# Queries spread into the score operand by transfers, expert choice and places later, in an attention and mixture-of-experts kernel

## The reference, cut to what matters

```
x = x + attention(layernorm(x), context)        # 16 heads of 16 channels; q and k are rms-normalised
x = x + experts(layernorm(x))                   # 8 experts, the best 2 of each token

probs = softmax(layernorm(x) @ gate_w.T); topw, sel = top_k(probs, 2); topw /= sum(topw)
out   = sum over the 2 chosen experts of topw * (silu(g) * u) @ w2,   g, u = split(x @ w1, 2)
```

## Time and profile before

| what | us |
|---|---|
| median of 3 runs (541.93 to 543.87) | 543.46 |
| the profiled execution's own time | 539.4 |
| its span | 537.6 |
| attention part with all engines in step, 59 to 302 us of the span | 243 |
| draining and the plan, to the first load of a slot at 340.89 | 39 |
| expert part, to about 505 | 164 |
| last stage | 33 |

### The profile page before, as it was taken

The page is one execution under the profiler, slowest core; times in us unless marked ns, Lnnn a source line. Parts: engine busy times, 40 slices in busy tenths (PEclk is TensorE's granted clock), DMA queues, the critical chain, the costliest instruction groups (busy, mean ns, idle before and its releaser), DMA issues.

```text
span 537.6 us, 14646 instructions
## 1 busy us (share of the span) xinstructions
PE 435.5 (81%) x4120; PEld 390.2 (73%) x4120; DVE 413.3 (77%) x1359; ACT 320.1 (60%) x934; POOL 303.4 (56%) x531
## 2 busy tenths in 40 slices
PE   1879899899999999999999861499999999999100
PEld 1668778787877887788878651399999999998000
DVE  7448998999999999999998965176777776766384
ACT  5367778777876787777777620265656666565000
POOL 6634377777777777777776646134445443544200
PEclk9879999999999999999999985599999999999655
DMA  7231442222222222223231114524344343431599
GB/s 225 65 113 43 132 142 75 81 79 80 78 75 82 75 84 74 85 65 89 68 95 53 51 41 129 148 73 131 116 124 130 116 128 119 122 116 60 182 404 351
DMA packets 49559, 60.51 MB, mean 113 GB/s; under 512 B 7615, under 2 KB 43082, under 8 KB 49482
## 3 DMA queue, kind: packets, MB, share of 16 engines
q1 hardware_dynamic: 38026, 38.00, 24.3%
q0 software_dynamic: 6528, 16.86, 9.1%
q10 hardware_dynamic: 4928, 4.72, 2.5%
HBM read 32.86 MB, written 23.27 MB: 104 GB/s over the span
## 4 chain that ended last, share of the span: by engine, by line
PE 68%; DVE 13%; DMA 5%; issue 5%; POOL 3%; SPq 3%; ACT 2%; POOLq 0%; DVEq 0%; ACTq 0%
PE bank L1117 13%; PE bank L1118 11%; PE bank L1119 11%; PE bank L1335 4%; DMA we_l<-expert_out 4%; PE bank L1125 3%; PE bank L1177 3%; PE bank L1231 2%; PE bank L1227 2%; PE bank L1229 2%; PE bank L1228 2%; PE bank L1150 2%; DVE late L835 2%; PE bank L1364 2%; PE bank L1365 2%
## 5 line engine op out<-in xcount | busy, mean ns | idle before, releaser
L527 POOL DMA_INDIRECT expert_out<-probs,late x72 | 70.0, 972 | 93.1 <-ACT probs L720 92.0
L457 POOL DMA_INDIRECT sorted_rows<-row,place_i x64 | 65.9, 1030 | 36.2 <-POOL row L451 25.3
L564 ACT CAST qp_h<-bank 32x256 f16<-32x256 f32 x128 | 46.4, 363 | 31.4 <-PE bank L1150 29.0
L841 DVE TENSOR_TENSOR qp_l<-bank,qp_h 32x256 f16<-32x256 f32 x128 | 52.9, 413 | 4.9 <-ACT qp_h L564 1.9
L1117 PE MATMUL bank<-we_h,xt_h 128*128 x144 | 53.6, 372 | 0.1
L1075 DVE SCALAR_TENSOR_TENSOR probs<-xn,late,bank 128x128 f32<-128x128 f32 x72 | 25.0, 348 | 35.6 <-ACT xn L708 35.6
L708 ACT ACTIVATE xn<-bank 128x176 f32<-128x176 f32 x72 | 22.8, 317 | 42.0 <-PE bank L1119 42.0
L1118 PE MATMUL bank<-we_l,xt_h 128*128 x144 | 47.2, 328 | 0.0
L1119 PE MATMUL bank<-we_h,xt_l 128*128 x144 | 47.1, 327 | 0.0
L1067 DVE TENSOR_TENSOR xt_l<-bank,xt_h 128x256 fp32r<-128x256 f32 x72 | 30.6, 425 | 20.3 <-ACT xt_h L702 16.1
L1335 PE MATMUL bank<-ident,late 128*128 128x128 f32 x144 | 30.7, 296 | 17.4 <-DMA late<-sorted_rows 15.7
(11 more groups left out here) (199 smaller groups left out, 1602.5 us busy)
## 6 DMA issues: line engine op xcount, KB each, us to landing
late<-sorted_rows SPq DMA_DIRECT2D x72, 129.0 KB, 2.1
we_f<-w_exp SPq DMA_DIRECT2D x32, 152.0 KB, 2.4
v_bd<-v_sb SPq DMA_DIRECT2D x128, 34.0 KB, 1.9
ctx_in<-ctx_t SPq DMA_DIRECT2D x32, 128.0 KB, 2.3
we_h<-expert_out SPq DMA_DIRECT2D x8, 512.0 KB, 6.8
we_l<-expert_out SPq DMA_DIRECT2D x8, 512.0 KB, 15.5
x<-x SPq DMA_DIRECT2D x3, 1024.0 KB, 5.8
out<-we_h ACTq DMA_DIRECT2D x8, 256.0 KB, 13.0
```

What stands on the lines that cost most here:

```text
L457: pool.indirect_dma_start(sorted_rows, bass.IndirectOffsetOnAxis(ap=place_i[:, t.slot // 2, k, t.par:t.par + 1], axis=0), row[:, k, t.slot ...
L527: pool.indirect_dma_start(expert_out, bass.IndirectOffsetOnAxis(ap=hs[:, r, D:D + 1].bitcast(U32), axis=0), y_sb[:, r % YRING, :], None, b ...
L564: act.copy(q_part(qp_h, t, g), q_bank(g)).then_inc(S["q_h_ready"], 1)
L841: dve.tensor_tensor(q_part(qp_l, t, g), q_bank(g), q_part(qp_h, t, g), ALU.subtract).then_inc(S["q_l_ready"], 1)
```

## The change

The four-part writes of `q_hi` and `q_lo` become one instruction each, of 128 partitions and 256 elements, into a new buffer `q_hl`; SyncE then spreads high and low part together with four transfers, one per group, into the score operand, whose order of dimensions is new. `score_max` waits for these transfers and has 16 matmuls with 64 stationary columns each in place of 8 with 128. On VectorE the negated maxima come straight behind `find_max`, `q_lo` comes ahead of `normalise` and of layer norm 1's statistics, `choose` moves from the end of an even turn into the middle of the following odd turn, and `route` one turn on. On TensorE `count_rows`, on GpSimd `send` and on SyncE `spread_v` come one turn later too, and the pipeline has one turn more. The comments on engines in the diff are added here.

```diff
-LAST = NT + 6
+LAST = NT + 7
...
-    qp_h = sb("qp_h", [P, 2, NB, KC, NQ, L], F16)
-    qp_l = sb("qp_l", [P, 2, NB, KC, NQ, L], F16)
+    qp = sb("qp", [P, 2, NQ, 2, KC, NB, L], F16)
+    q_hl = sb("q_hl", [P, 2, D], F16)
...
+        def spread_q(t):                       # SyncE
+            need_alone(sp, sp_passed, S["q_l_ready"], t.n + 1)
+            need_alone(sp, sp_passed, S["scored"], t.n - 1)
+            if t.n == 0:
+                sp.wait_ge(q_cleared, 1)
+            for g in range(NQ):
+                part = slice(g * 2 * HD, (g + 1) * 2 * HD)
+                sp.dma_start(qp[part, t.par, g, :, :, :, :].rearrange("p n c b l -> p (n c b l)"),
+                             q_hl[part, :, :].rearrange("p n x -> p (n x)")).then_inc(q_spread[t.par], 16)
...
         def turn(j, s):                        # SyncE
+            if Tile(j, s - 1).live:
+                spread_q(Tile(j, s - 1))
             if Tile(j, s + 2).live:
                 load_ctx(Tile(j, s + 2))
             if Tile(j, s + 1).live and (not isinstance(j, int) or j * SKEW + s + 1 >= 2):
                 load_weights(Tile(j, s + 1))
-            if Tile(j, s).live:
-                spread_v(Tile(j, s))
+            if Tile(j, s - 1).live:
+                spread_v(Tile(j, s - 1))
...
-            if Tile(j, s - 6).live:            # GpSimd
-                send(Tile(j, s - 6))
+            if Tile(j, s - 7).live:
+                send(Tile(j, s - 7))
...
         def q_hi(t):                           # ScalarE
             act.wait_ge(S["q_transposed"], t.n + 1)
-            if t.first:
-                act.wait_ge(q_cleared, 2)
-            need(act, S["scored"], t.n - 1)
-            for g in range(NQ):
-                act.copy(q_part(qp_h, t, g), q_bank(g)).then_inc(S["q_h_ready"], 1)
+            if t.n >= 1:
+                act.wait_ge(q_spread[1 - t.par], (t.n + 1) // 2 * 16 * NQ)
+            act.copy(q_hl[:, 0, :], kq_bank[:, 0:D]).then_inc(S["q_h_ready"], 1)
...
         def q_lo(t):                           # VectorE
-            dve.wait_ge(S["q_h_ready"], NQ * t.n + NQ)
-            need(dve, S["scored"], t.n - 1)
-            for g in range(NQ):
-                dve.tensor_tensor(q_part(qp_l, t, g), q_bank(g), q_part(qp_h, t, g), ALU.subtract
-                                  ).then_inc(S["q_l_ready"], 1)
+            dve.wait_ge(S["q_h_ready"], t.n + 1)
+            dve.tensor_tensor(q_hl[:, 1, :], kq_bank[:, 0:D], q_hl[:, 0, :], ALU.subtract
+                              ).then_inc(S["q_l_ready"], 1)
...
                 find_max(tile(2))              # VectorE's turn
-            if ahead:
-                n = j * SKEW + s + 2 if isinstance(j, int) else None
-                ln1_stats(ahead, {2: x_second, 8: x_third, 9: x_rest}.get(n))
-            if tile(2).live:
                 neg_max_hi(tile(2))
             if tile(3).live:
                 invert_sums(tile(3))
             if tile(2).live:
                 neg_max_lo(tile(2))
+            if tile(1).live:
+                q_lo(tile(1))
             if tile(3).live:
                 normalise(tile(3))
             if ahead:
+                n = j * SKEW + s + 2 if isinstance(j, int) else None
+                ln1_stats(ahead, {2: x_second, 8: x_third, 9: x_rest}.get(n))
                 ln1_mean(ahead)
-            if tile(1).live:
-                q_lo(tile(1))
             if tile(4).live:
                 ln2_norm(tile(4))
             if tile(3).live:
                 att_lo(tile(3))
             if s % 2 == 1 and tile(5).live:
-                route(tile(5), tile(4), (s - 5) // 2 % 2)
+                a = tile(5)
+                a.first = isinstance(j, int) and a.n == 0
+                choose(a, tile(4), (s - 5) // 2 % 2)
+            if s % 2 == 0 and tile(6).live:
+                route(tile(6), tile(5), (s - 6) // 2 % 2)
...
-            if s % 2 == 0 and tile(4).live:    # last in VectorE's turn, behind residual
-                a = tile(4)
-                a.first = isinstance(j, int) and a.n == 0
-                choose(a, tile(3), (s - 4) // 2 % 2)
...
-            pe.wait_ge(S["q_h_ready"], NQ * t.n + NQ)        # score_max, TensorE
+            pe.wait_ge(q_spread[t.par], (t.twins + 1) * 16 * NQ)
...
-                        ins = pe.matmul(score_bank[:, at:at + P], flat(qp_h[:, t.par, b, c, 2 * gh:2 * gh + 2, :]),
-                                        flat(kp[:, t.par, 0, b, c, :, :]), start=True, stop=True)
+                        for m in range(2):
+                            ins = pe.matmul(score_bank[m * L:(m + 1) * L, at:at + P], qp[:, t.par, 2 * gh + m, 0, c, b, :],
+                                            flat(kp[:, t.par, 0, b, c, :, :]), start=True, stop=True)
...
-            pe.wait_ge(S["q_l_ready"], NQ * t.n + NQ)        # score
...
-                    q_h, q_l = (flat(q[:, t.par, b, c, :, :]) for q in (qp_h, qp_l))
+                    q_h, q_l = (qp[:, t.par, :, n, c, b, :] for n in range(2))
...
-            if s % 2 == 1 and tile(5).live:                  # TensorE's turn
-                count_rows(tile(5).pair, (s - 5) // 2 % 2, static and i == 5)
+            if s % 2 == 0 and tile(6).live:
+                count_rows(tile(6).pair, (s - 6) // 2 % 2, static and i == 6)
```

More of the change, by code:

```diff
@@ L224, in k_parts @@
         return kp[:, t.par, part].rearrange("p b c q l -> p (c q) b l")
[L226 to L231, removed]
     x_first, x_second, x_third, x_rest = sem("x_first"), sem("x_second"), sem("x_third"), sem("x_rest")
@@ L239, in build_in @@
     we_loaded = [sem(f"we_loaded{p}") for p in range(2)]
+    q_spread = [sem(f"q_spread{p}") for p in range(2)]
     v_spread = [sem(f"v_spread{p}") for p in range(2)]
@@ L518, in _ @@
         assert done[0] == SETUP_POOL, done[0]
-        for q in (qp_h, qp_l):
-            pool.memset(q[:, :, :, :, :, :].rearrange("p u b c g l -> p (u b c g l)").bitcast(F32), 0.0
-                        ).then_inc(q_cleared, 1)
+        pool.memset(qp[:, :, :, :, :, :, :].rearrange("p u g n c b l -> p (u g n c b l)").bitcast(F32), 0.0
+                    ).then_inc(q_cleared, 1)
         turns_sp(pool, turn)
@@ L654, in turn @@
             if tile(1).live:
-                t = tile(1)
-                t.first = isinstance(j, int) and t.n == 0
-                q_hi(t)
+                q_hi(tile(1))
             if tile(2).live:
@@ L1129, in tr_x @@
             need(pe, S["xt_l_ready"], t.n)
-            if t.slot % 2 == 0:
+            if t.slot % 2 == 1:
                 need(pe, R["filled_new"], t.pair - 2)
@@ L1138, in tr_k @@
             pe.wait_ge(S["kn_ready"], t.n + 1)
-            need(pe, S["q_l_ready"], NQ * t.n)
+            need(pe, S["q_l_ready"], t.n)
             for c in range(KC):
```

## The result

The changed kernel took 549.3 us (median of 4 runs, 547.45 to 550.71), the kernel before, beside it, 543.7: a ratio of 1.0109, 95% interval 1.0071 to 1.0147. I had forecast 536.3, between 530 and 543. The forecast was wrong, and so was its side.

A forecast was written before the change was run, and what follows sets the result against it. TensorE was taken to bound one turn and VectorE the other. Two turns save 0.60 us, 13.5 times: -8.1; filling +0.5, draining +0.4: -7.2 us, from 543.46 to 536.3, range 530 to 543.

The forecast's parts named there:

- layer norm 1's mean: On VectorE, the mean comes 0.65 us later; GpSimd's two turns then take 17.45 us, just below TensorE's 17.56.
- my sum: GpSimd's loop over two turns, counted from `tr_k`: 6.6 + 8.05 + 1.15 + 1.65 = 17.45 us.
- Choice: `choose` in the odd turn's middle is covered, so `k_lo` is in time and TensorE's 18.4 us of waits go.
- `score_max`: On TensorE, 16 narrow matmuls in place of 8 cost +0.45 us a turn, other end 0.
- Maxima: Maxima negated straight behind `find_max` end TensorE's wait at `tr_max`: -0.11 us a turn.
- Transfers: SyncE's query transfers land 1.9 us after issue, hidden ahead of `score_max` with 0.2 to 0.7 us to spare: 0 us.
- Filling: While the pipeline fills, one longer `score_max` falls on the path: +0.5 us.
- Draining: At the pipeline's end, clock kept -1.7 us, one more `send` +3.25: sum +0.4, bounds -1 and +3.5.
- GpSimd's idle bits: Rival: the 0.24 to 0.29 us before GpSimd's L413 are sequencer work, no waits; 542.5 us, chance 0.15.
- two turns at 17.9 or more: Sign against the forecast: two turns stay at 17.9 us or more with GpSimd full; forecast 17.5.
- GpSimd with hardly an idle bit other than for layer norm 1's mean: Sign for the forecast: GpSimd's only remaining idle time of note is its wait for that mean.

The follow-up runs named there:

- e17: The changed kernel without further edit, run a third time, on chip E: 538.5 us, ratio 0.9965 to before.
- e18: The changed kernel with layer norm 1's statistics straight behind `find_max` and `q_lo` behind the mean, as before, on chip E: 533.3 us, ratio 0.9859.
- e5: The kernel before, unchanged, profiled once more on chip B: one run, 542.98 us.
- e14: The changed kernel with the front half of VectorE's turn as before and `weights_lo` ahead of `send`, on chip D: ratio 1.0185 to before.
- e1: The kernel before with only `score_max` changed to 16 matmuls of 64 stationary columns, on chip A: ratio 1.0067.
- e3: The kernel before with only `choose`, `route`, `count_rows` and `send` placed later as in the changed kernel, on chip A: ratio 0.9960.
- e4: The changed kernel with `spread_v` back at its old place in SyncE's order, on chip A: 556.5 us, ratio 1.0246 to before.
- e11: The changed kernel with `q_lo` back behind layer norm 1's mean, on chip C: 535.6 us, ratio 0.9931 to before.
- e15: The kernel of e14 profiled once more: one run, 551.82 us.
- e6 to e8: `send` moved last in GpSimd's turn, in the changed kernel, the kernel before, and the kernel of e3, on chip B: ratios 1.0904, 1.0429, 1.1114 to before.
- e12: The changed kernel with the front half of VectorE's turn as before, the same edit as e18, on chip C: 535.0 us, ratio 0.9914 to before.
- e10: The kernel before with `weights_lo` ahead of `send` in GpSimd's turn, on chip C: ratio 1.0006.
- e13: The changed kernel without further edit, run again on chip D: 550.4 us, ratio 1.0171 to before.

## Why the prediction was wrong, step by step

**The step that failed** is the one on layer norm 1's mean: "Count from the start of `tr_k` at 139.17: `qk_rms` at 145.76 is 6.6 us in". The size of the delay was right, 0.60 us measured (3.09 - 2.49) for 0.65. What was wrong is the point that I counted from. In the profile of before TensorE was busy, and `tr_k` started at 139.17, 1.20 us behind the start of `k_scale`, which ScalarE's timeline of before has at 137.97:

```profile
137.97 0.47 ACT L628 ACTIVATE late<-bank,r_qk 128x256 f32<-128x256 f32 x1 [0.43 <-POOL r_qk L415]
```

Once TensorE is not the bound, `tr_k` starts 0.53 behind `k_scale`, but `find_max` doesn't come earlier: it starts 3.50 behind `k_scale` in before (141.47 - 137.97) and 3.51 in e17. So the loop doesn't go through the start of `tr_k`. It goes from `k_scale` through the work behind it on ScalarE (softmax, `row_copy`, `e_gap`, `k_hi`) to `k_lo`, `xt_lo` and `find_max`. One turn of that loop in e17, ScalarE, VectorE and GpSimd:

```profile
136.31 0.47 ACT L631 ACTIVATE late<-bank,r_qk 128x256 f32<-128x256 f32 x1 [1.83 <-POOL r_qk L421]
145.22 0.47 ACT L631 ACTIVATE late<-bank,r_qk 128x256 f32<-128x256 f32 x1 [0.98 <-POOL r_qk L421]
154.61 0.47 ACT L631 ACTIVATE late<-bank,r_qk 128x256 f32<-128x256 f32 x1 [1.50 <-POOL r_qk L421]
```

```profile
139.82 1.22 DVE L845 TENSOR_REDUCE bank<-bank 128x16 f32<-128x1024 f32 x1
```

```profile
142.90 0.22 POOL L419 TENSOR_SCALAR veps<-mean_var 128x1 f32<-128x1 f32 x1 [0.87 <-DVE mean_var L825]
144.20 0.19 POOL L419 TENSOR_SCALAR ms_eps<-sumsq 128x2 f32<-128x2 f32 x1
...
152.26 0.19 POOL L419 TENSOR_SCALAR veps<-mean_var 128x1 f32<-128x1 f32 x1
...
153.54 0.22 POOL L419 TENSOR_SCALAR ms_eps<-sumsq 128x2 f32<-128x2 f32 x1
```

`k_scale` to `find_max` 3.51, to the mean at GpSimd 3.08, to `qk_rms` 1.30, to the next `k_scale` 1.02: 8.91 us. The next turn, 145.22 to 154.61, is GpSimd's own, 9.39.

In the terms of my sum, from `tr_k` at 136.84 to `tr_k` at 155.14: 7.36 to `qk_rms` at 144.20, where I had 6.6; 8.06 to the next layer norm, where I had 8.05; 1.28 to its `qk_rms` for 1.15; 1.60 to `tr_k` for 1.65. That is 18.30 us for my 17.45, and the first term makes 0.77 of the difference: 0.67 by the start (0.53 in place of 1.20), 0.15 by 1.30 for the layer norm in place of 1.15, less 0.06 by 3.08 for the mean in place of 3.14. The mean over ten pairs is 18.27, against the 17.56 that I forecast. Over 13.5 pairs of turns that is 9.6 us, more than the whole gain that I had forecast.

The turns show the same. Before has 8.54 us from `k_scale` at 137.97 to that at 146.51, and so 9.62 for the turn with `choose` at its end. After the change these are 8.91 and 9.39 in e17: what the moved choice gives, the later mean takes back. With the old order the first is 8.47, and two are 17.82 (e18).

**Late signals** were no step of mine: the only profile that I had shows none. One sign was there, and I carried it over without asking for its cause: the median of the runs of before lay 4 us above the profiled execution, about what late signals cost that kernel (3.6). That they are those 4 us isn't shown. They turn e17's 0.35% gain into the loss of the result, as after's `k_scale` shows, with turns of 9.52 and 9.20 us:

```profile
148.52 0.47 ACT L631 ACTIVATE late<-bank,r_qk 128x256 f32<-128x256 f32 x1 [0.73 <-POOL r_qk L421]
158.04 0.47 ACT L631 ACTIVATE late<-bank,r_qk 128x256 f32<-128x256 f32 x1 [1.34 <-POOL r_qk L421]
167.24 0.47 ACT L631 ACTIVATE late<-bank,r_qk 128x256 f32<-128x256 f32 x1 [0.73 <-POOL r_qk L421]
```

Why the changed kernel loses 12 us by them and before 3.6 is shown in part. ScalarE's `k_scale` in e5:

```profile
156.16 0.48 ACT L628 ACTIVATE late<-bank,r_qk 128x256 f32<-128x256 f32 x1 [0.44 <-POOL r_qk L415]
164.97 0.47 ACT L628 ACTIVATE late<-bank,r_qk 128x256 f32<-128x256 f32 x1 [0.44 <-POOL r_qk L415]
174.60 0.47 ACT L628 ACTIVATE late<-bank,r_qk 128x256 f32<-128x256 f32 x1 [0.43 <-POOL r_qk L415]
```

Its turns are 8.81 and 9.63. The one with `choose` at its end takes as long as in before without late signals (9.62), for VectorE is busy without a break with `choose`, `k_lo` and `xt_lo` up to `find_max`, 2.4 us behind the end of `score_max`, longer than its signal is ever late there (1.4); only the other turn can grow. In after no `choose` covers it, and both grow. Besides, in after `q_hi` starts 1.73 behind the end of `tr_q`, and behind it in VectorE's queue stand `q_lo` and the mean (at GpSimd 155.65, 5.59 behind `score_max`; in e17 161.20 - 156.15 = 5.05). But e14, with the mean ahead of `q_lo`, loses as much, and e1, whose narrow matmuls cost 0.02 us a turn by themselves (below), has 18.59 for two turns against e5's 18.30. What else is in it stays open.

The other steps:
- **Choice**: right on the waits. 18.4 us became 0.9 (e3) and 0.2 (after); e17 has 3.9, 12 times 0.3, for a `k_lo` that itself waits for ScalarE and no longer stands behind `choose`. Alone it did not shorten the turns (e3).
- **`score_max`**: +0.45 a turn was wrong, the other end of my bounds right. e1 shows it alone, since its `tr_x` (L1134) is as in before:

```profile
149.32 0.38 PE L1134 MATMUL bank<-ident,xn 128*128 128x128 f32 x2
149.63 0.64 PE L1166 MATMUL bank<-late,qp_h 128*64 128x128 f16 x16
150.10 1.07 PE L1178 MATMUL bank<-v_bd,probs 128*64 128x34 f32 x32
```

From `score_max` to `weigh` 16 narrow matmuls take 0.47 us where the eight took 0.54, from `tr_x` to `score_max` it is 0.31 where before has 0.22 (147.82 to 148.04): +0.02 a turn in all. By the Trainium skill, page "TensorEngine Tiling (Array Packing)", section "Key Properties", different tiles run weight loads and matmuls in parallel, and a change of the tiling mode drains the engine. The trace agrees with both: twice as many matmuls take no longer, and the 0.09 us move from ahead of `weigh`, where before changes its mode, to ahead of `score_max`, where after does.
- **Maxima**: right. e17's bias product starts at 159.66 and `tr_max` at 159.89, 0.23 apart where before had 0.34.

```profile
155.14 0.66 PE L1140 MATMUL bank<-ident,late 128*128 128x128 f32 x4 [0.55 <-ACT late L631]
...
156.15 0.64 PE L1163 MATMUL bank<-late,qp 128*64 128x128 f16 x16
...
159.66 0.39 PE L1122 MATMUL bank<-bias_hl,ones_row 128*128 128x512 f32 x1
159.89 0.23 PE L1204 MATMUL bank<-ident_b,neg_max 128*128 128x128 bf16 x1
```

- **Transfers**: right in the kernel as changed, 1.9 us to landing (e17) and 0.6 us of waits in all; e4 and e11 show how little is left.
- **Filling**: wrong. Tile 9's keys come 2.2 us earlier in e17, not 0.5 later: before the first sends two turns take 17.2 to 17.4 us, less than the loop above allows with them.
- **Draining**: from tile 29's keys to the first slot 57.6 us against 56.55, +1.0 for my +0.4, within its bounds. TensorE's idle time shrank as forecast, from 2.55 to 1.33 us, but the clock was not kept: the granted clock was 0.50 from 305.4 to 308.7 us in e17, as long as behind the idle time in before, so the -1.7 did not come.
- **GpSimd's idle bits** (my first rival): waits, at least at `qk_rms`. In e17 it starts 1.30 behind the layer norm with no idle time shown, in before 1.45 with 0.26.

One sign that I had named did come, two turns at 17.9 or more. The other, "GpSimd with hardly an idle bit other than for layer norm 1's mean", could not tell my case from this one: that bit is the loop.

## What to carry to other kernels

Count a loop from the instruction that releases it, not from one that the present bound holds back: what such an instruction shows as distance is slack of the old bound. When an engine's order is changed, follow every result that comes later by it, here a mean of 0.18 us that stands ahead of GpSimd's work, and not only the engine that the profile shows busy. And before explaining a difference of a per cent, profile the kernel before on the same chip: two profiles of one file differed here by more than the change.

## What the runs showed of the hardware

**Late completion signals of TensorE.** On chips A, B and D and in the first profile of after, signals of `score_max`, `weigh` and `tr_q` came up to 2.3 us (after) and 2.7 us (e15) behind the recorded end in nearly every turn in which `send`'s indirect transfers were issued beside them. With the transfers elsewhere (e6 to e8, on B) they were in time. On C and E some came up to 0.7 us late (e12), and in the first profile of before all were there within 0.03. The transfers stand beside the same matmuls in e17 as in after, so that place alone does not make the signals late. Records go with it: a complete profile of before has 10,595 semaphore events (first profile, and e10 on C), e5 has 8,549; the changed kernel has 11,901 in e17, 8,916 in its first profile and 8,860 in e13.

By the Trainium skill, page "NOTIFIC — the notification-queue block", section "7.1 Overflow: three behaviours, one of which stalls the engine", the block that writes such records holds its producers back rather than lose one inside it, and a queue in memory may be told to drop what doesn't fit. Lost records and late signals on the same chips fit that, but e6 to e8 lost records (10,244, 7,427 and 7,613 are left) and had these signals in time, so neither is shown to cause the other. Whether an execution that records nothing has late signals, and what sets these chips apart, no run here can show; that the timed runs differ between the chips as their profiles do is shown by 550.4 and 538.5 us.
